# Row table copied ahead of the tile experts with its own signal, place numbers written as whole numbers, second mixture tile turned halfway through the first

## The reference, cut to what matters

```
top1_idx = jnp.argmax(probs, axis=-1)
order = jnp.lexsort((-top1_prob, top1_idx))
pos_in_group = jnp.arange(T) - start[sorted_e]
keep_sorted = pos_in_group < capacity
final_e = jnp.where(keep, top1_idx, 0)
...
h = relu(tokens @ W1[e] + b1[e]);  y = h @ W2[e] + b2[e]      # 256 -> 1024 -> 256
out = out + jnp.where((final_e == e)[:, None], y, 0.0)
```

## Time and profile before

| | |
|---|---|
| median of 3 runs | 589.93 us (588.35 to 590.24) |
| the profiled execution's own time | 590.48 us |
| its span, first to last instruction | 588.7 us |
| granted TensorE clock, mean | 0.997 |
| PE, PEld, DVE, ACT, POOL busy | 94%, 78%, 54%, 41%, 40% |
| chain that ended last: PE, POOL, DVE, issue, DMA, ACT | 71%, 13%, 6%, 5%, 3%, 2% |

### The profile page before, as it was taken

One profiled execution on the slowest core, in us unless ns is written; L12 is line 12 of the kernel. 1 busy time (PEld: TensorE's weight loads), 2 busy tenths in 40 slices (PEclk: granted clock), 3 DMA queues, 4 the chain that ended last, 5 costly groups with the idle time before them and its releaser, 6 DMA issues.

```text
span 588.7 us, 11475 instructions
## 1 busy us (share of the span) xinstructions
PE 553.5 (94%) x3809; PEld 461.1 (78%) x3809; DVE 318.2 (54%) x965; ACT 242.1 (41%) x669; POOL 233.9 (40%) x319
## 2 busy tenths in 40 slices
PE   3899999988999999999999999999999998997895
PEld 3788887744999999988888978888888886775664
DVE  2777767677222225743447764444444445766564
ACT  1555444660211111115544245555555454443432
POOL 1512211042111121006635375555555078777860
PEclk9999999999999999999999999999999999999998
DMA  5980000185995532513396025655555233655552
GB/s 131 336 363 3 1 1 2 63 362 241 322 327 184 181 114 72 154 55 74 81 282 220 1 83 161 162 161 161 157 158 158 78 91 110 192 179 162 159 181 75
DMA packets 53207, 88.31 MB, mean 150 GB/s; under 512 B 11250, under 2 KB 43891, under 8 KB 51604
## 3 DMA queue, kind: packets, MB, share of 16 engines
q1 hardware_dynamic: 45028, 65.29, 32.0%
q0 software_dynamic: 8112, 22.16, 15.8%
HBM read 62.38 MB, written 25.04 MB: 149 GB/s over the span
## 4 chain that ended last, share of the span: by engine, by line
PE 71%; POOL 13%; DVE 6%; issue 5%; DMA 3%; ACT 2%; SPq 0%; POOLq 0%; ACTq 0%; DVEq 0%
POOL arena L917 11%; PE psum L1558 10%; PE psum L1314 10%; PE psum L1325 9%; PE psum L1470 7%; PE psum L1572 6%; PE psum L1170 5%; PE psum L1142 5%; PE psum L1487 3%; PE psum L1550 3%; POOL iota_i L947 2%; PE psum L1150 2%; PE psum L1505 1%; PE psum L1566 1%; PE psum L1164 1%
## 5 line engine op out<-in xcount | busy, mean ns | idle before, releaser
L917 POOL DMA_INDIRECT arena<-x,row_tok x71 | 68.1, 959 | 52.7 <-PE psum L1550 43.0
L917 POOL DMA_INDIRECT arena<-y_sorted,pos_k_i x64 | 64.9, 1015 | 36.5 <-DMA y_sorted<-arena 16.3
L1558 PE MATMUL psum<-big_w,arena 128*128 x284 | 72.9, 379 | 0.0
L1633 PE MATMUL psum<-big_w,arena 128*128 x256 | 62.9, 379 | 0.0
L1871 ACT ACTIVATE arena<-psum,arena 128x128 f32<-128x128 f32 x64 | 18.2, 368 | 108.1 <-PE psum L1314 85.8
L1314 PEld LDWEIGHTS psum<-arena,big_w 128*128 128x128 f32 x512 | 59.5, 192 | 2.7 <-issue 1.0
L1314 PE MATMUL psum<-arena,big_w 128*128 128x128 f32 x512 | 59.9, 275 | 1.5 <-DVE arena L2558 1.5
L1470 PE MATMUL psum<-arena,big_w 128*128 128x256 f32 x256 | 59.9, 381 | 0.2 <-ACT arena L1890 0.2
L1558 PEld LDWEIGHTS psum<-big_w,arena 128*128 128x128 f32 x284 | 53.7, 190 | 7.2
L1325 PE MATMUL psum<-arena 128*128 128x256 f32 (+1 forms) x256 | 57.7, 379 | 0.0
L2794 DVE SCALAR_TENSOR_TENSOR arena<-arena 128x128 f32<-128x128 f32 x71 | 20.8, 293 | 59.6 <-ACT arena L1957 58.2
(11 more groups left out here) (327 smaller groups left out, 989.1 us busy)
## 6 DMA issues: line engine op xcount, KB each, us to landing
y_sorted<-arena SPq DMA_DIRECT2D x71, 128.0 KB
big_w<-w SPq DMA_DIRECT2D x8, 1024.0 KB, 5.1
tokens<-x SPq DMA_DIRECT2D x4, 1024.0 KB, 14.5
x<-tokens SPq DMA_DIRECT2D x16, 256.0 KB, 2.6
z_kept<-arena SPq DMA_DIRECT2D x16, 256.0 KB
out<-arena SPq DMA_DIRECT2D x16, 256.0 KB
y_late<-arena SPq DMA_DIRECT2D x16, 128.0 KB, 1.7
big_w<-expert_w_t SPq DMA_DIRECT2D x1, 2048.0 KB, 7.8
```

Of the source, the lines that this page charges most:

```text
L917: pool.indirect_dma_start(dst, None, rows, bass.IndirectOffsetOnAxis(ap=idx, axis=0)).then_inc(done, 16)
L1558: mm = pe.matmul(bank[2 + i % RT][:, 0:2 * M1], c_gt[i % RT][:, k, :], mgu_s[:, k, bass.ds(e, 1), :].rearrange("p a m -> p (a m)"), start= ...
L1633: mm = pe.matmul(o, z_t[u][:, k, n * P:(n + 1) * P], ew_s[:, k, bass.ds(e, 1), :].rearrange("p a d -> p (a d)"), start=False, stop=n == NB ...
```

## The change

Seven edits, all within routing, table and the tile experts:

- The whole-number place is computed by the same instruction as the float one, from its inputs, instead of copied from its result. The float one is no longer linked.
- The copy of the table to `row_tok` moves ahead of the reduction for `tile_e`, behind a wait for PE's table products. It signals `l_in` (to 4) instead of `table`.
- POOL waits for `l_in` >= 4 instead of `table` >= 1.
- `table` is now signalled by the last of the two copies into `pos_i`.
- The idle products behind the table's products are 18 instead of 21.
- `g_t` has two buffers, used in turn; the second takes its place from a gap in the arena.
- PE turns tile 1's rows halfway through up 0 (behind its first 16 products) instead of after it. The order for later tiles is as before.

```
-        g_t = G.take(KD, P)
+        g_t = [G.take(KD, P)]
         act_t = [G.take(NF, P) for _ in range(2)]
-        G.at += FF
+        g_t.append(G.take(KD, P))
+        G.at += FF - KD * P
...
                 pool.wait_ge(l_hs, 48)
-                pool.wait_ge(table, 1)
+                pool.wait_ge(l_in, 4)
                 gathers(TILES_L, h_late, True)
...
                 mm.then_inc(tab_ps, 1)
-                idle_products(21)
+                idle_products(18)
...
-            def expert_up(i):
+            def expert_up(i, halfway=None):
...
-                        mm = pe.matmul(..., big_w[:, c:c + P], g_t[:, k, :],
+                        mm = pe.matmul(..., big_w[:, c:c + P], g_t[u][:, k, :],
                                        start=k == 0, stop=k == KD - 1)
                     if f == NF // 2 - 1:
                         mm.then_inc(up_half, 1)
+                        if halfway:
+                            halfway()
...
-                    expert_up(i)
-                    if i + 1 < tiles:
-                        rows_in(i + 1, (i + 1) % 2, (i + 1) // 2)
+                    if i == 0:
+                        expert_up(0, lambda: rows_in(1, 1, 0))
+                    else:
+                        expert_up(i)
+                        if i + 1 < tiles:
+                            rows_in(i + 1, (i + 1) % 2, (i + 1) // 2)
...
-                link(dve.scalar_tensor_tensor(pos_l, fin_l, float(P), rank_l, ALU.mult, ALU.add))
-                link(dve.tensor_copy(pos_li, pos_l))
+                dve.scalar_tensor_tensor(pos_l, fin_l, float(P), rank_l, ALU.mult, ALU.add)
+                link(dve.scalar_tensor_tensor(pos_li, fin_l, float(P), rank_l, ALU.mult, ALU.add))
...
                 link(dve.tensor_tensor(tcmp_l, ..., ALU.is_ge))
+                dve.wait_ge(tab_ps, 1)
+                dve.tensor_copy(row_tok[:, 0:TILES_L], bank[3][:, 0:TILES_L]).then_inc(l_in, 1)
                 link(dve.tensor_reduce(tile_fl, tcmp_l, AXX, ALU.add))
                 dve.tensor_copy(tile_e[:, E0:TILES_L], tile_fl[:, E0:])
                 dve.tensor_copy(tile_e[:, 0:E0], iota_f[:, 0:E0])
...
                 for t in range(2):
-                    dve.tensor_copy(odd[P - QL:P, :, t], pos_l[t * QL:(t + 1) * QL, :])
-                dve.wait_ge(tab_ps, 1)
-                dve.tensor_copy(row_tok[:, 0:TILES_L], bank[3][:, 0:TILES_L]).then_inc(table, 1)
+                    m = dve.tensor_copy(odd[P - QL:P, :, t], pos_l[t * QL:(t + 1) * QL, :])
+                m.then_inc(table, 1)
...
-            def scale_rows(i):
+            def scale_rows(i, u):
                 dve.wait_ge(g_ps, i + 1 + 2)
                 for k in range(KD):
-                    m = dve.tensor_scalar(g_t[:, k, :], bank[0][:, k * P:(k + 1) * P], gout[:, k:k + 1], None, ALU.mult)
+                    m = dve.tensor_scalar(g_t[u][:, k, :], bank[0][:, k * P:(k + 1) * P], gout[:, k:k + 1], None, ALU.mult)
                 m.then_inc(g_ev, 1)
```

More of the change, by code:

```diff
@@ L1313, in expert_up @@
                         c = at + k * FF + f * P
-                        mm = pe.matmul(bank[1 + 2 * u + f // 4][:, (f % 4) * P:(f % 4 + 1) * P], big_w[:, c:c + P], g_t[:, k, :],
+                        mm = pe.matmul(bank[1 + 2 * u + f // 4][:, (f % 4) * P:(f % 4 + 1) * P], big_w[:, c:c + P], g_t[u][:, k, :],
                                        start=k == 0, stop=k == KD - 1)
@@ L2593, in experts @@
                 loops = E0 // 2 if late else (tiles - 2) // 2
-                scale_rows(0)
-                scale_rows(1)
+                scale_rows(0, 0)
+                scale_rows(1, 1)
                 dve.wait_ge(ld_b, 32)
@@ L2600, in experts @@
                         e = relu_half(i - 1, v)
-                        scale_rows(i + 1)
+                        scale_rows(i + 1, v)
                         add_bias(i - 1, v, e, r)
@@ L2605, in experts @@
                     if i + 1 < tiles:
-                        scale_rows(i + 1)
+                        scale_rows(i + 1, (i + 1) % 2)
                     if late and i == min(NULL_UNITS):
```

## The result

The changed kernel took 587.29 us (median of 7 runs, 586.55 to 588.17) against 589.93 (7 runs, 588.35 to 591.93): ratio 0.9959, 95% interval 0.9940 to 0.9977. That is 2.6 us off the median (2.4 by the ratio) where 1.57 was forecast; the forecast time was 588.4, in a range from 587.3 to 590.1, and 587.29 lies at its lower end. Two more comparisons of the same two kernels gave 0.9968 (0.9949 to 0.9986) and 0.9983 (0.9967 to 0.9999). All three intervals hold the forecast's 1 - 1.57/590 = 0.9973. The profiled execution took 587.29 us, its span was 585.6, so 3.1 less than before's 588.7. What has to be explained is thus whether the forecast 1.57 came in its own steps, and what the rest is.

A forecast was written before the change was run, and what follows sets the result against it. PE's own work was taken to bound the kernel from tile 2 on, so any earlier start passes through whole. Front 0.71 plus second tile 0.86 gives 1.57 us off the median 589.93: 588.4 us, range 587.3 to 590.1.

The forecast's parts named there:

- The bound: PE never idle from tile 2 on; ahead of that, gather 0's landing releases the first transposes, idle products 0.2 us behind.
- Whole-number place, 0.12: On DVE ahead of the table: unlinking the float place brings one-hots, table products and all behind them 0.12 us earlier.
- Table copy, 0.71: On DVE: the copy moved ahead of the reduction signals POOL 0.71 us earlier, the 0.12 included; later `table` costs 0.
- POOL's 0.88 stays: POOL still starts gather 0 0.88 us after the table copy's end, so at 141.90, landing at 144.80.
- first rival: POOL starts gather 0 0.27 us after its signal, idle products then decide, front gives about 1.0 us: 588.1 us; 15%.
- Front, 0.71: Up to up 0: first transposes move from 145.61 to 144.90, up 0 to 146.10, a gain of 0.71 us.
- Second tile, 0.86: Between up 0 and up 1: DVE's scaling runs beside up 0's remaining products, so up 1 gains 0.86 us more.
- What is late next: After up 1: tile 0's relu has 1.1 us slack, gather 2 lands at 153.1 against 153.65; nothing costs.
- DVE's block beside the first gather: First gather takes 1.19 us on POOL, later ones 0.95 and 0.94; the added 0.25 us is paid before and after.
- second rival: The front doesn't move: DVE's block holds gather 0, or gather 2 lands late; gain 0.7 to 0.9 us, 589.2; 16%.
- third: PE blocks mid up 0 on a gather 1 that takes 7.5 us and stands 2.97 us: 591.3 us; 5%.
- fourth rival: Nothing comes through: gain lost in tile 0's relu or a later stage that hangs on a transfer: 589.9 us; 5%.

The follow-up runs named there:

- front_only: The changed kernel with tile 1's rows turned after up 0, as before the change; 588.72 us, ratio 0.9985 to the kernel before.
- quiet_dve: The changed kernel with one more wait: DVE starts its block of 12 small instructions only when gather 0 has landed; 592.48 us, one run.
- wait_first_18: The changed kernel with POOL's wait for the table copy written ahead of the one for the stored rows, 18 idle products kept; 588.57 us, one run.
- wait_first_16: The changed kernel with POOL's same two waits swapped and 16 idle products instead of 18; 587.83 us, ratio 0.9968 to the kernel before.
- idle_21: The changed kernel with 21 idle products again instead of 18; 590.6 us, one run.
- before_again: The kernel before, unedited, run for a second trace; 588.95 us, one run.
- after_again: The changed kernel, unedited, run for a second trace; 587.90 us (12 runs), ratio 0.9968 to the kernel before.
- after_third: The changed kernel, unedited, run once more beside wait_first_16_again on the same chip; 588.61 us, ratio 0.9983 to the kernel before.
- halfway_only: The changed kernel with the table's part undone and 21 idle products, tile 1 still turned halfway through up 0; 588.19 us, ratio 0.9979 to the kernel before.
- wait_first_16_again: wait_first_16 repeated unchanged, beside after_third on the same chip; 587.39 us, ratio 0.9966 to the kernel before.

## Why the prediction was right, point by point

**The bound.** PE from tile 2 on, never idle: held. What down 0 gained arrived at 342 us whole, in the first pair 1.49 and then 1.60. The first transposes released by gather 0's landing, idle products just behind: held, SP's bias load and the transposes 0.02 apart in both.

**Whole-number place, 0.12.** Held: the table's products start at 7.33 instead of 7.46 and 7.45.

**Table copy, 0.71.** A little too large: it was 0.65 (8.75 to 8.10), the 0.12 included. The copy starts 0.10 us behind the end of the table's products (140.85 to 140.95), where the prediction let it start 0.03 behind. `table` later, nobody late for it: held.

**POOL's 0.88 stays.** Held in all traces of the changed kernel, to 0.01. The reason given against the first rival, that the quick gathers follow closely on others, was wrong: the quick ones carry the wait that matters (gather 2 waits for `g_ps` itself and starts 0.27 behind the transposes), and the first gather is as quick once it carries it (0.29 us behind the copy, three traces). The rival's condition was one swapped pair of lines away, and with it the transposes came at 11.74 against 12.19, 0.45 us.

**Front, 0.71.** It was 0.61 on the mean of three traces (0.56, 0.65, 0.61), and 0.67 in front_only. Of the 0.10 that is missing 0.06 is the copy's; the rest lies in the time between the gather's start and its landing, which varied: from the first gather's start to SP's bias load it is 2.98 and 2.99 in the traces of before, 3.07, 2.99 and 3.03 in those of the changed kernel, 2.95 in front_only.

**Second tile, 0.86.** Held: up 1 gained (18.73 - 17.26) - 0.61 = 0.86 in the changed kernel. Missed: 0.1 us more inside up 1.

**Sum, 1.57.** Down 0 came 1.53, 1.62 and 1.58 us earlier in three traces. The mechanism came as said, but that the sum fits to 0.01 us is luck: a front 0.1 too large and a restart of 0.1 left out cancel.

**What is late next.** Nothing, as said: the relu of tile 0 and gather 2 were in time, down 0 stands directly behind its transposes.

**DVE's block beside the first gather.** The 0.25 us is paid before and after, as said. The block isn't what it comes from: with DVE silent beside it the gather takes no less (1.19 us, quiet_dve), and with the waits swapped it starts at 0.30 although DVE is at work (wait_first_18). No run has DVE silent between the copy and the gather's start, and none shows the block holding POOL back, as the second rival has it.

**The chances.** The prediction gave 37% to more than 0.3%, and the first comparison has 0.41%. By the traces the change itself is worth 1.58 us, 0.27%, which is what was put as just within; the other two comparisons have 0.32% and 0.17%. What the first median shows beyond the forecast is scatter as far as the traces tell. The second, third and fourth rival didn't happen: the first gather at 142.00 and not 142.6, no idle time in up 0, none before rows 2, and the gain still there at 342 us.

## What to carry to other kernels

Of the three waits ahead of this kernel's first gather on GpSimd, the gather carried the one written first, in all twelve traces. With the wait that is fulfilled last in that place the gather started 0.29 us behind the copy instead of 0.88 (wait_first_18, wait_first_16), which was worth 0.45 us in the traces, and 0.58 with two idle products fewer, at a place where moving the producer ahead by two thirds of a microsecond took four edits. So where several waits stand ahead of a gather, swapping their lines is worth a try, and the gather's record in the trace tells which one it waits for. A gain of 0.3% is read from distances to a common event shortly ahead of it in the traces, where executions agree to 0.1 us, and not from two spans, which differ by 1.5 us for the kernel before and by 2.6 for the changed one. And where idle products cover a wait, their number has to follow the wait when it shrinks: three too many cost 0.20 us here (idle_21).

## What the runs showed of the hardware that was not expected

Of the three waits written ahead of the first gather, the first stands in the gather's own record and the other two in a separate one (semaphores 149, and 167 with 164, in before; 158, and 167 with 149, in wait_first_18; likewise in all twelve traces). From the end of the copy to the gather's start it is 0.88 us where the copy's signal is waited for in the separate record (before, before_again, after, after_again, after_third, front_only, halfway_only, idle_21, quiet_dve), and 0.29 where the gather waits for it (wait_first_18, wait_first_16, wait_first_16_again). PE's first two products behind the gap ahead of up 1 start 0.213 us apart (before, before_again, front_only), behind the one ahead of up 0 0.184 (all twelve), instead of 0.112. The first gather takes 1.19 us on POOL and the next one 0.95, whether DVE works beside it (before, after) or not (quiet_dve). An idle time of PE of 2.41 us ahead of up 0 was followed by 3.41 us at a granted clock of 0.50 (quiet_dve); one of 0.79 or 0.80 was not (the other eleven traces, 1.00 there).
